# Local attention layers of a fused kernel: scores and output products taken for two slots at a time

## What is computed

```python
def local_attention(q, k, v):          # b, 16 heads, n tokens, 64
    bq = q.reshape(b, h, nw, w, d)     # w = 32
    bk2, bv2 = (look(bk), look(bv))    # own window and the one before: 64 keys
    mask = (it < jb) | (it > jb + w) | (jb == -1)
    sim = jnp.einsum('bhwie,bhwje->bhwij', bq, bk2) * QK_SCALE
    sim = jnp.where(mask, -jnp.finfo(sim.dtype).max, sim)
    attn = jax.nn.softmax(sim, -1)
    out = jnp.einsum('bhwij,bhwje->bhwie', attn, bv2)

def attn_layer(x, Wqkv, qs, ksc, Wo):
    q, k, v = jnp.split(x @ Wqkv, 3, -1)
    q = l2norm(q) * qs; k = l2norm(k) * ksc
    q = q * cos * scale + rotate_half(q) * sin * scale
    k = k * cos * inv + rotate_half(k) * sin * inv
    return local_attention(q, k, v) @ Wo

def ffn_layer(x, g, bln, W1, b1, W2, b2):
    xn = (x - mu) / jnp.sqrt(var + 1e-05) * g + bln
    a, gate = jnp.split(xn @ W1 + b1, 2, -1)
    return a * jax.nn.gelu(gate, approximate=False) @ W2 + b2

for i in range(6):
    x = attn_layer(shift_tokens(x), ...) + x
    x = ffn_layer(shift_tokens(x), ...) + x
```

## Time and profile before

| | before |
|---|---|
| median of 3 runs | 2562.83 us (2562.13 to 2564.97) |
| the profiled execution | 2564.41 us |
| its span, first to last instruction | 2562.6 us |
| TensorE busy, share of the span | 94% |
| VectorE, ScalarE, GpSimd | 78%, 74%, 69% |
| mean granted TensorE clock | 0.986 |
| the slots of the local layers | from 529 to about 2206 us |

### The profile page before, as it was taken

One profiled execution on the slowest core, in us unless ns is written; L12 is line 12 of the kernel. 1 busy time (PEld: TensorE's weight loads), 2 busy tenths in 40 slices (PEclk: granted clock), 3 DMA queues, 4 the chain that ended last, 5 costly groups with the idle time before them and its releaser, 6 DMA issues.

```text
span 2562.6 us, 98064 instructions
## 1 busy us (share of the span) xinstructions
PE 2408.3 (94%) x36437; PEld 1707.2 (67%) x36441; DVE 2006.5 (78%) x4387; ACT 1884.9 (74%) x6630; POOL 1764.7 (69%) x1605
## 2 busy tenths in 40 slices
PE   6999777879999999999999999999999999789999
PEld 5888544446666666666666666666667666368874
DVE  5555699978888888888888888888888888555644
ACT  4777788858888888888888888888888888433323
POOL 1888886568888888888888888888888888122200
PEclk9999999999999999999999999999999999799999
DMA  4101210021112111111112111211121111100000
GB/s 121 15 15 15 50 13 12 11 76 36 33 33 62 37 42 33 53 46 41 33 35 65 42 33 33 62 39 41 33 56 44 41 33 34 30 1 1 1 1 17
DMA packets 176292, 91.06 MB, mean 36 GB/s; under 512 B 40926, under 2 KB 172232, under 8 KB 175824
## 3 DMA queue, kind: packets, MB, share of 16 engines
q1 hardware_dynamic: 167200, 80.50, 11.6%
q0 software_dynamic: 8192, 4.21, 1.4%
q10 hardware_dynamic: 432, 0.07, 0.0%
HBM read 30.57 MB, written 3.76 MB: 13 GB/s over the span
## 4 chain that ended last, share of the span: by engine, by line
PE 82%; DVE 11%; issue 4%; POOL 2%; ACT 1%; SPq 1%; DMA 0%; DVEq 0%; POOLq 0%; ACTq 0%
PE bank L1114 13%; PE bank L1131 9%; PE scores L1166 7%; PE bank L1177 7%; PE bank L1121 6%; PE scores L1148 6%; DVE rg_prod L952 3%; PE bank L1103 3%; PE bank L1206 3%; PE bank L626 2%; PE bank L1224 2%; PE bank L1215 2%; PE scores L1142 2%; PE scores L654 2%; PE bank L667 1%
## 5 line engine op out<-in xcount | busy, mean ns | idle before, releaser
L1550 POOL TENSOR_TENSOR rs<-ssc,neg_half 128x8 f32<-128x8 f32 x384 | 643.6, 1676 | 41.1 <-DVE ssc L1370 41.1
L1540 POOL TENSOR_TENSOR t_pair<-qn_pair,tabs 128x512 f32<-128x512 f32 x384 | 488.8, 1273 | 12.3 <-DVE qn_pair L1358 11.6
L1478 ACT ACTIVATE pr<-scores,negmax 128x64 f32<-128x64 f32 x1536 | 460.3, 311 | 49.3 <-DVE negmax L1378 24.3
L1530 POOL TENSOR_TENSOR pr<-pr,rec 128x256 f32<-128x256 f32 x384 | 235.1, 612 | 282.8 <-DVE rec L1350 282.7
L1114 PE MATMUL bank<-wqk,xs 128*128 128x512 f32 x768 | 402.6, 606 | 12.5 <-DVE qn_pair L1358 11.4
L1013 POOL DMA_INDIRECT rg_win<-rg_images,share_down x256 | 257.5, 1006 | 91.6 <-issue 57.5
L1478 ACT ACTIVATION_READ_ACCUMULATOR pr<-scores,negmax 128x1 f32 x1536 | 311.2, 203 | 0.0
L1366 DVE TENSOR_REDUCE ss<-sq 128x8 f32<-128x512 f32 x384 | 261.4, 681 | 33.2 <-ACT sq L1501 32.1
L1358 DVE TENSOR_TENSOR qn_pair<-bank,rs 128x512 f32<-128x512 f32 x384 | 258.0, 672 | 27.2 <-POOL rs L1550 27.0
L1469 ACT COPY vt<-bank 128x256 f32<-128x256 f32 x361 | 135.1, 374 | 188.5 <-issue 187.3
L1331 DVE TENSOR_TENSOR qr_pair<-t_pair 128x512 f32<-128x512 f32 x384 | 266.4, 694 | 0.2 <-issue 0.2
(11 more groups left out here) (307 smaller groups left out, 5490.2 us busy)
## 6 DMA issues: line engine op xcount, KB each, us to landing
rg_prod<-vt SPq DMA_DIRECT2D x1536, 32.0 KB, 1.9
wqk<-in_L_ffn_Wqkv SPq DMA_DIRECT2D x20, 256.0 KB
rg_win<-rg_images,share_down POOLq DMA_INDIRECT x256
wv<-in_L_ffn_Wqkv SPq DMA_DIRECT2D x20, 128.0 KB
wo<-in_L_ffn_Wo SPq DMA_DIRECT2D x20, 128.0 KB, 2.4
w<-in_L_ffn_W SPq DMA_DIRECT2D x6, 341.0 KB
rg_images<-rg_prod SPq DMA_DIRECT2D x1, 1625.0 KB, 8.4
rg_images<-XT SPq DMA_DIRECT2D x16, 64.0 KB, 1.5
```

The lines of the kernel that those rows point to most:

```text
L1478: ex = act.activation(pr[t % 2][:, h * BAND:(h + 1) * BAND], sl_ps[:, h // 2, h % 2 * BAND:(h % 2 + 1) * BAND], ACT.Exp, bias=negmax[t % 2 ...
L1540: pool.tensor_tensor(t2[t % 2][:, :].rearrange("p (i h f e) -> p i h f e", i=2, h=GH, f=2), qn[t % 2][:, :].rearrange("p (i h f e) -> p i ...
L1550: pool.tensor_tensor(rs[t % 2][:, :], ssc[t % 2][:, :], neg_half[:, 0:8], ALU.pow)\
```

## The change

Scores and output products are made in odd slots only, for two items each. Slot u, odd, scores items u-7 and u-6 (L_SCORE 7) with one mask product per bank over both, and makes output products of items u-11 and u-10 (L_ATTEND 11). The scores take 256 columns of each bank, the output products the other 256. In the even slot after it VectorE takes one maximum over both items (negmax_pair), after the norm; ScalarE copies both outputs at once to oT, and both items are projected (L_OUT 12). Exponentials stay one item per slot (L_EXP 8). In even slots ScalarE's order is now: oT copy, vt copy, pT copy, squares, exponentials, shift of xs, FFN, qkT copy; in odd slots: vt copy, exponentials, pT copy, squares, FFN, qkT copy. Reciprocal and scaling get a lag of their own (L_REC 9). qkT, xs have three buffers, vt and its second tile four, probabilities four halves of the two tiles. LATER and its put-off projections go. L_PROJ rises to 11, so FFN_FIRST is 27, and two slots are added.

```diff
-L_QKV, L_ROPE, L_COS, L_SUM, L_TURN, L_SCORE, L_V, L_MOVE, L_EXP, L_PROB, L_PROJ = 1, 2, 3, 4, 5, 6, 5, 6, 7, 8, 9
+L_QKV, L_ROPE, L_COS, L_SUM, L_TURN, L_V, L_MOVE, L_EXP, L_REC, L_PROB, L_PROJ = 1, 2, 3, 4, 5, 7, 8, 8, 9, 10, 11
+L_SCORE, L_ATTEND, L_OUT = 7, 11, 12
...
-LATER = {0: (1, 2), 1: (2, 1), 8: (10, 0), 9: (10, 1)}
...
-        sl_ps, ol_ps = scores[:, :, 0:P], scores[:, :, P:2 * P]
+        sl_ps = scores[:, :, 0:2 * P].rearrange("p r (i k) -> p r i k", i=2)
+        ol_ps = scores[:, :, 2 * P:4 * P].rearrange("p c (i n) -> p c i n", i=2)
...
+        xs = [sb(f"xs{i}", [P, P]) for i in range(3)]
...
+        negmax_pair = sb("negmax_pair", [P, 2 * GH])
...
+        vx = [rg_flat[1][:, 6 * CW + i * GV:6 * CW + (i + 1) * GV] for i in range(4)]
...
+        qkT_local = qkT + [e_spare[:, 13 * F:14 * F]]
+        pr_local = [pr[i % 2][:, i // 2 * GB:(i // 2 + 1) * GB] for i in range(4)]
...
-                    near, far = vt[t % 3], vx[t % 2]
+                    near, far = vt[t % 4], vx[t % 4]
                     sp.wait_ge(a.v_moved, TICKS + t + 1)
-                    sp.wait_ge(a.o_ready, TICKS + t - 1)
+                    if t >= 4:
+                        sp.wait_ge(a.o_ready, TICKS + t - 3)
...
+        def pair_at(u, lag):
+
+            return (u - lag, u - lag + 1) if (u - lag) % 2 == 0 and live(u - lag) else None
+
+        def through(t):
+
+            return TICKS + min(max(t, 0), LOCAL)
 
...
-                pe.wait_ge(a.qkT_moved, TICKS + t + 1)
-                pe.wait_ge(a.exp_ready, TICKS + t)
-                if live(u - 1 - L_PROB):
-                    pe.wait_ge(a.oT_moved, TICKS + u - L_PROB)
-                st = qkT[t % 2]
+            def score(pair_, u):
+                pe.wait_ge(a.qkT_moved, TICKS + pair_[1] + 1)
                 for r in range(2):
-                    pe.matmul(sl_ps[:, r, :].rearrange("p (a k) -> p a k", a=2), ident16[:, :],
-                              over(local_mask[:, :], [P, 2, BAND], 1), start=True, stop=False, skip_group_check=True)
-                for pair in range(2):
-                    for key, lo in BLOCKS:
+                    pe.matmul(sl_ps[:, r, :, :].rearrange("p i (a k) -> p (i a) k", a=2), ident16[:, :],
+                              over(local_mask[:, :], [P, 4, BAND], 1), start=True, stop=False, skip_group_check=True)
...
+                                row = slice(r * HD, (r + 1) * HD)
+                                mm = pe.matmul(sl_ps[lo:lo + WINDOW, r, t % 2, pair * BAND:(pair + 1) * BAND],
+                                               st[row, pair * P + lo:pair * P + lo + WINDOW],
+                                               st[row, (2 + pair) * P + key:(2 + pair) * P + key + BAND],
+                                               start=False, stop=True, skip_group_check=True)
+                mm.then_inc(a.sc_ready, 2)
+
+            def attend(pair_):
+                pe.wait_ge(a.pT_moved, TICKS + pair_[1] + 1)
+                for t in pair_:
+                    pe.wait_ge(a.v_spread[t % 2], 64 * (t // 2 + 1))
+                    for k, (_, lo, hi) in enumerate(SPANS):
                         for r in range(2):
-                            row = slice(r * HD, (r + 1) * HD)
-                            mm = pe.matmul(sl_ps[lo:lo + WINDOW, r, pair * BAND:(pair + 1) * BAND],
-                                           st[row, pair * P + lo:pair * P + lo + WINDOW],
-                                           st[row, (2 + pair) * P + key:(2 + pair) * P + key + BAND],
-                                           start=False, stop=True, skip_group_check=True)
-                mm.then_inc(a.sc_ready, 1)
-
-            def attend(t, u):
-                pe.wait_ge(a.pT_moved, TICKS + t + 1)
-                pe.wait_ge(a.v_spread[t % 2], 64 * (t // 2 + 1))
-                pe.wait_ge(a.oT_moved, TICKS + t)
-                if live(u - L_EXP):
-                    pe.wait_ge(a.exp_ready, TICKS + u - L_EXP + 1)
-                for k, (_, lo, hi) in enumerate(SPANS):
-                    for r in range(2):
-                        for pair in range(2):
-                            row = slice(pair * HD, (pair + 1) * HD)
-                            at = SLOT_V[k][pair] * P + r * HD
-                            values = vt[t % 3] if k == 2 * pair else vx[t % 2]
-                            mm = pe.matmul(ol_ps[r * HD:(r + 1) * HD, pair, lo:hi], values[row, at:at + HD],
-                                           pT[t % 2][row, r * P + lo:r * P + hi],
-                                           start=True, stop=True, skip_group_check=True)
-                mm.then_inc(a.o_ready, 1)
+                            for pair in range(2):
+                                row = slice(pair * HD, (pair + 1) * HD)
+                                at = SLOT_V[k][pair] * P + r * HD
+                                values = vt[t % 4] if k == 2 * pair else vx[t % 4]
+                                mm = pe.matmul(ol_ps[r * HD:(r + 1) * HD, pair, t % 2, lo:hi], values[row, at:at + HD],
+                                               pT[t % 2][row, r * P + lo:r * P + hi],
+                                               start=True, stop=True, skip_group_check=True)
+                mm.then_inc(a.o_ready, 2)
+
+            def tiles(u):
+                scored, attended = pair_at(u, L_SCORE), pair_at(u, L_ATTEND)
+                if scored or attended:
+                    pe.wait_ge(a.exp_ready, through(u - L_SCORE))
+                    pe.wait_ge(a.oT_moved, through(u - L_ATTEND))
+                if scored:
...
                     queries(u - L_QKV)
                 if live(u - L_PROB):
                     turn_probs(u - L_PROB, u)
-                for t in projections(u, 0):
-                    project(t)
                 if live(u - L_TURN):
                     turn_queries(u - L_TURN)
-                for t in projections(u, 1):
-                    project(t)
                 c, step = ffn_step(u)
                 if c is not None:
                     ffn(c, step)
                     down(c, 2)
                 if live(u - L_V):
                     values(u - L_V)
-                if live(u - L_SCORE):
-                    score(u - L_SCORE, u)
-                if live(u - L_PROB):
-                    attend(u - L_PROB, u)
-                for t in projections(u, 2):
+                tiles(u)
+                for t in pair_at(u, L_OUT) or ():
                     project(t)
             for u in range(TAIL):
...
+            def maximum(u):
+                scored = pair_at(u, L_SCORE)
+                if scored:
+                    dve.wait_ge(a.sc_ready, TICKS + scored[1] + 1)
+                    dve.wait_ge(a.oT_moved, through(u - L_ATTEND + 2))
+                    dve.wait_ge(a.exp_ready, TICKS + scored[0])
+                    dve.tensor_reduce(negmax_pair[:, :].rearrange("p (r i a) -> p r (i a)", r=2, i=2),
+                                      sl_ps.rearrange("p r i (a k) -> p r (i a) k", a=2), AX.X, ALU.max, negate=True)\
+                        .then_inc(a.negmax_ready, 2)
 
...
-                t = u - L_PROJ
-                if live(t) and bursts(u - 1):
-                    b, g = t // GROUPS, t % GROUPS
-                    dve.wait_ge(a.o_ready, TICKS + t + 1)
+                attended = pair_at(u, L_OUT)
+                if attended and bursts(u - 1):
+                    b, g = attended[0] // GROUPS, attended[0] % GROUPS
+                    dve.wait_ge(a.o_ready, TICKS + attended[1] + 1)
                     if g == 0:
-                        dve.wait_ge(a.y_ready, B + max(t - GROUPS, 0))
-                    dve.tensor_copy(oT[b % 2][:, g * GV:(g + 1) * GV].rearrange("p (c n) -> p c n", c=2), ol_ps)\
-                        .then_inc(a.oT_moved, 1)
+                        dve.wait_ge(a.y_ready, B + max(attended[0] - GROUPS, 0))
+                    dve.tensor_copy(oT[b % 2][:, g * GV:(g + 2) * GV].rearrange("p (i c n) -> p i c n", i=2, c=2),
+                                    ol_ps.rearrange("p c i n -> p i c n")).then_inc(a.oT_moved, 2)
                 if bursts(u - 1):
                     pT_copy(u - L_PROB)
                 c, step = ffn_step(u - 1)
...
+                inverse(u - L_REC)
+                normed(u - L_ROPE)
+                maximum(u - 1)
                 t = u - L_TURN
                 if live(t) and bursts(u):
                     dve.wait_ge(a.qkT_ready, t + 1)
-                    dve.wait_ge(a.sc_ready, TICKS + t - 1)
-                    dve.tensor_copy(qkT[t % 2][:, :], turn_ps[:, :]).then_inc(a.qkT_moved, 1)
+                    dve.wait_ge(a.sc_ready, TICKS + t - 2)
+                    dve.tensor_copy(qkT_local[t % 3][:, :], turn_ps[:, :]).then_inc(a.qkT_moved, 1)
                 t = u - L_V
                 if live(t) and bursts(u):
                     dve.wait_ge(a.v_ready, TICKS + t + 1)
-                    dve.wait_ge(a.o_ready, TICKS + t - 2)
```

(60 more changed lines are left out.)

63 lines of the change are left out of this document (21 added, 42 removed).

## The result

The changed kernel takes 2739.45 us (median of 4 runs, 2734.09 to 2744.26), the kernel before beside it 2563.74 us. The ratio is 1.0691, with a 95% interval of 1.0676 to 1.0705: slower by 176 us, where the forecast was slower by 40 (2603, in a range of 2550 to 2635). The profiled run of the changed kernel took 2744.26 us, with a span of 2742.5.

What follows compares the result with a forecast made beforehand. Round trips through ScalarE, VectorE and GpSimd were taken to bind most pairs: a period of 70.42 us against 69.1, +33 over the stage, +7.9 at its end, together +41, giving 2603 us, range 2550 to 2635.

Steps and rivals of the forecast that it cites:

- light slots: Slots without an FFN product: 3.93 us now, bound by the round trip through ScalarE and VectorE, against 3.58 of TensorE work.
- shift, spread and burst: Shift of xs every fourth slot, 0.64 us; FFN spread step, 0.64 more in its pair; Gelu burst, where VectorE takes over copies.
- Loop 2: Round trip per pair through VectorE and GpSimd, from second exponentials over sum, rs, norm and maximum to the next: 8.06 us.
- to VectorE's norm 1.67: Step from the start of GpSimd's rs to VectorE's norm, priced at 1.67 us.
- Loop 1: Round trip per pair through ScalarE, from the even slot's queries to the next even slot's: 7.98 us.
- turned probabilities start at 0.97: On TensorE, 0.97 us after the even slot's queries start: 0.86 for the queries plus 0.11.
- 0.62 instead of 0.78: TensorE's paired score block per pair, in us; part of a total TensorE saving of 0.52 per pair.
- 0.80: TensorE's paired output products: 0.80 us per pair instead of 0.96.
- 15-0: Pair of slots at FFN steps 15 and 0, forecast bound by TensorE at 8.36 us.
- Rival 4: TensorE, idle in light pairs, gets 1.2 instead of 2.4 GHz there; two such pairs a period: +290 us, chance 0.02.
- +7.9: The stage ends two slots later, at least 3.93 us each with the last groups running out.
- Rival 3: An engine's lateness carries into the next pair, from GpSimd's scaling holding up rs: +38 us, 2641, chance 0.08.

Runs made afterwards that it cites:

- three reorderings on ScalarE and VectorE: Each alone against the changed kernel: vt copy ahead of output copy, 2722.38 us; maximum ahead of norm, 2701.70; shift of xs in odd slots, 2698.84.
- filler run: Changed kernel plus one unused 128x128 VectorE reduction ahead of the rotation sum in slots without much FFN work: 2743.96 us, ratio 1.0711.
- later versions: Changed kernel with four reorderings together, ratio 1.0141, and versions built on it with the even slots' turned probabilities ahead of the queries, 0.9996 to 1.0092.

## Why the prediction was right in sign and wrong in size

**Right:** that the light slots are bound by round trips and not by TensorE, that both loops close once per pair, that shift, spread and burst stand in them. The three reorderings on ScalarE and VectorE moved the pairs they should, and both loops measure the same 8.50 us. The mechanism was right; what failed are terms of the sum, the largest of which is the first below.

**Loop 2, the term "to VectorE's norm 1.67".** It was 2.10. The prediction took rs from the earlier trace rows, where VectorE's maximum (L1378) stood behind the sum of squares while rs began. The text notes that the change moves the maximum away, but not what then stands in its place: the rotation sum. With two inputs in SBUF it delays rs by what is left of it: 629.60 + 0.43 = 630.03, and the next operation of VectorE starts at 630.09. Of the 107 rs of the changed kernel that began under a rotation sum 106 were long; of the 149 rs of the kernel before that began under the maximum none was. The Trainium skill has this rule ("SBUF — State Buffer", Who interferes with whom): an instruction of VectorE with two inputs in SBUF and a GpSimd instruction that reads SBUF share a port, and the one that comes second waits until the first is finished. The trace agrees where the rotation sum comes first. It does not the other way round: in the filler run rs came first by 0.04 us and kept its 1.64, but the sum did not wait for it either and took 0.72. The prediction did not weigh any of this. Of 384 rs 128 were long, 21 of them 3.3 us; before, 33 and none over 2.1.

The 3.3 us are in part open. Those rs end as if they had waited for the rotation sum and the cosines as well (710.41 + 1.66 = 712.07, and the operation behind the cosines starts at 712.13), although both began after rs did. All 21 began under the last up step, which has 85 rows and takes one of its two large inputs from PSUM. The 36 that began under an up step of 128 rows took 1.64, with the same two operations behind it (705.81 in the rows above). Why the 85 rows make the difference no run tested.

**Loop 1, "turned probabilities start at 0.97".** They started at 1.20. They wait for ScalarE's vt copy, as both tiles lie in bank 4, and in even slots that copy now stands behind the paired output copy (622.78 + 0.38). The prediction named bank 4 for the value product and forgot it for the probabilities. With the vt copy first they start at 0.96.

**TensorE's blocks, "0.62 instead of 0.78" and "0.80".** The paired score block takes 0.79 (628.99 to 629.78) and the output products 0.83. Loop 1 is thus 8.50 = 7.98 + 0.23 + 0.17 + 0.03 and about 0.1 in ScalarE's steps. Two sets of 32 scores cost no less than twice one, so the saving per pair was not 0.52 but 0.3: 2.14 - (0.31 + 0.79 + 0.83) = 0.21, and about 0.1 at the projection. The price was worked out from the pace of the first 32 records, 0.45 - 0.22. In the paired block the first 32 keep it (0.46 - 0.22 = 0.24 us), but the second 32 take 0.59 - 0.22 = 0.37. Why they are slower is not shown.

**The pairs.** These terms are 3.84 us a period, 85 us. Worst was 15-0, "8.36, TensorE": it took 9.26, since the long rs at the last up step makes the norm, and the maximum behind it, late (with the maximum ahead 8.80).

**What was not in the sum at all:** the stops in the run of small products, 27 us, which the run that cuts that run in two took away almost whole. Rival 4, the clock, came to a small part of its price: 12 stretches at half clock rather than two light pairs a period. They and the stops are almost all of the 53 us of the irregular part, 32 in the pairs with a stop and 19 in other pairs at half clock; the 19 hold some waits of TensorE too, and no run changed the clock alone.

**The drain, "+7.9".** It was nothing: 388.8 us behind the last queries in both kernels. Which work covers the two slots more was not followed up.

**Rival 3** (lateness carried on, 2641) was the nearest in size, but its mechanism did not show: rs was released by VectorE's second reduction (218.4 of 221.3 us idle, in the page), not held up by the scaling. All told, the stage: 33 forecast + 8 in the slots ahead of the FFN (119 instead of 111) + 85 + 53 = 179, against 1824.7 - 1644.7 = 180 in the profiled runs.

## What to carry to other kernels

Pairing tiles to save an engine's fixed costs makes every single buffer between the engines a round trip per pair, so first write down each trip and see which steps of other engines stand between its two ends. When an operation is moved away, ask what its neighbours now run beside: here the mover left a GpSimd step under a two-input VectorE operation. If two trips have the same length, one fix at a time shows nothing on the plain case; try them together before giving one up.

## What the runs showed of the hardware

A GpSimd operation of 128x8 that takes 1.64 us took 2.07 to 2.10 in 106 of the 107 cases in which it began under a rotation sum of VectorE, and kept 1.64 when it began 0.04 us before one. Under an up step of 85 rows it took 3.30 in all 21 cases (2.93 to 3.16 in the later versions), under one of 128 rows 1.64 in all 36. TensorE stopped 22 times for up to 1.7 us without a semaphore in runs of 112 small products and their weight loads, and 6 times once a value product of 0.44 us stood in the middle. A stage in which TensorE waited about a tenth of the time was granted 1.2 GHz in 12 stretches, each behind an idle time of 1.4 to 1.9 us, where the fuller one had none.
